# A transformer block on one core: the transposed input comes from TensorE, and every engine's order of work is rewritten

## What is computed

```
q, k, v = LN(x) @ Wq, LN(x) @ Wk, LN(x) @ Wv
P       = softmax(mask(q @ k.T) / 16)            # causal
x       = x + LN((P @ v) @ Wo)
i       = argmax(log_softmax(logits) + gumbel(u))   # one of 8 weights
x       = x + LN(LN(x) @ W[i] + b[i])
```

## Time and profile before

| | |
|---|---|
| median of three runs | 430.8 us |
| profiled execution | 428.95 us |
| its span, first to last instruction | 427.1 us |
| mean granted clock of TensorE | 0.975 |
| busy | PE 90%, DVE 77%, ACT 61%, POOL 51% |
| data moved | 67.75 MB, 159 GB/s |

### The profile page before, as it was taken

One profiled execution on the slowest core, in us unless ns is written; L12 is line 12 of the kernel. 1 busy time (PEld: TensorE's weight loads), 2 busy tenths in 40 slices (PEclk: granted clock), 3 DMA queues, 4 the chain that ended last, 5 costly groups with the idle time before them and its releaser, 6 DMA issues.

```text
span 427.1 us, 7846 instructions
## 1 busy us (share of the span) xinstructions
PE 384.1 (90%) x2652; PEld 359.5 (84%) x2652; DVE 330.9 (77%) x844; ACT 259.3 (61%) x642; POOL 216.0 (51%) x367
## 2 busy tenths in 40 slices
PE   7996967999869998999879998799979998999994
PEld 6775856999769996899769997699968997899994
DVE  4488755799847987789867998579868998667876
ACT  5866555576546665575655765567665757555642
POOL 5115264554645554645855446455656448535234
PEclk9998998999989998999999999899999999999998
DMA  6323884249843498328872498435982388331012
GB/s 196 119 55 122 240 221 115 69 171 254 229 130 103 193 240 238 115 69 271 232 190 81 163 262 243 126 114 199 272 219 82 120 241 237 105 107 51 25 51 74
DMA packets 45611, 67.75 MB, mean 159 GB/s; under 512 B 8196, under 2 KB 38276, under 8 KB 44676
## 3 DMA queue, kind: packets, MB, share of 16 engines
...
q10 hardware_dynamic: 272, 0.26, 0.2%
...
## 4 chain that ended last, share of the span: by engine, by line
PE 45%; DMA 26%; issue 9%; DVE 7%; ACT 4%; POOL 3%; POOLq 3%; SPq 3%; DVEq 0%
PE bank L1003 25%; PE score L1003 17%; DMA p_kept<-p_turn 16%; DMA p_turn<-p_kept 9%; ACT pT_hi L704 3%; SPq L443 3%; PE bank L1157 2%; POOLq L517 2%; DVE p_turn L911 2%; POOL pT_lo L546 1%; DMA x_kept<-x_turn 1%; DVE neg_scores L901 1%; DVE g_lo L767 1%; ACT g_hi L582 1%; PE bank L1128 1%
## 5 line engine op out<-in xcount | busy, mean ns | idle before, releaser
L546 POOL TENSOR_TENSOR pT_lo<-p_turn,pT_hi 128x128 fp32r<-128x128 f32 (+7 forms) x60 | 82.2, 1393 | 22.2 <-ACT pT_hi L704 22.1
L1003 PE MATMUL bank<-v_hi,pT_lo 128*128 128x258 f32 x288 | 82.6, 287 | 7.0 <-DVEq L865 3.9
L1003 PE MATMUL bank<-v_lo,pT_hi 128*128 128x258 f32 x288 | 81.6, 283 | 0.0
L1003 PE MATMUL bank<-v_hi,pT_hi 128*128 128x258 f32 x288 | 81.2, 282 | 0.0
L1003 PE MATMUL score<-xT_hi,g_lo 128*128 128x384 f32 (+4 forms) x176 | 65.0, 369 | 15.0 <-DVE neg_max L901 14.9
L503 POOL TENSOR_TENSOR o_rstd<-o_ss,minus_half 128x1 f32<-128x1 f32 x64 | 37.9, 594 | 77.4 <-ACT squares_junk L738 77.4
L695 ACT ACTIVATE probs<-neg_scores,neg_max 128x128 f32<-128x128 f32 (+3 forms) x64 | 49.2, 776 | 42.0 <-DVE neg_max L901 41.9
L1003 PE MATMUL score<-xT_hi,g_hi 128*128 128x384 f32 (+4 forms) x176 | 63.2, 359 | 0.0
L1003 PE MATMUL score<-xT_lo,g_hi 128*128 128x384 f32 (+4 forms) x176 | 63.2, 359 | 0.0
L1003 PEld LDWEIGHTS bank<-v_hi,pT_lo 128*128 128x128 f32 x288 | 54.7, 190 | 8.5 <-issue 6.9
L1003 PEld LDWEIGHTS bank<-v_lo,pT_hi 128*128 128x128 f32 x288 | 54.9, 191 | 0.6
...
## 6 DMA issues: line engine op xcount, KB each, us to landing
x_sb<-in_L_attn_x_dram SPq DMA_DIRECT2D x32, 256.0 KB, 5.4
out_dram<-f_sb SPq DMA_DIRECT2D x31, 256.0 KB, 5.6
x_kept<-x_turn SPq DMA_DIRECT2D x7, 1024.0 KB, 4.3
x_turn<-x_kept SPq DMA_DIRECT2D x28, 256.0 KB, 7.1
p_kept<-p_turn SPq DMA_DIRECT2D x7, 960.0 KB, 9.8
...
p_kept<-p_turn SPq DMA_DIRECT2D x7, 704.0 KB, 3.1
...
```

Source lines behind the costliest of these rows:

```text
L546: nc.gpsimd.tensor_tensor(p_half(pT_lo, n), p_quads(n), p_half(pT_hi, n).bitcast(f32), ALU.subtract).then_inc(p_lo_ready, 1)
L1003: last = nc.tensor.matmul(dst, l, r, start=(i == 0), stop=(i == len(passes) - 1))
```

## The change

X becomes a step of PE. For each pair of tiles of the next batch, four transposes with the identity go from `xn` into a PSUM bank; ACT rounds from there to `xT_hi`, DVE subtracts to `xT_lo` and releases the bank. The steps B, W and R go, and with them the DRAM tensor `x_kept` and the buffer `x_turn`. The jobs that share the four banks become 28 a batch. pT has four slots in place of three, numbered through the batches. G2 and G3 move behind S0 and S1 of the batch that uses them. The lists of all five engines are rewritten. The waits that counted whole batches now count the entries of the lists (`turned`, `rounded`, `reduced`), since the last batch has no block transposes for some tiles.

```diff
--- before.py
+++ after.py
@@ -54,10 +54,9 @@
-    PS = 3
+    PS = 4
...
-    PE_ORDER = """S0 S1 S2 S3 O6' O7' S4 Y1' V0 S5 Y2' F0' O0 S6 S7 O1 F1' V1 V2 Y3' F2' O2 V3 F3' O3 O4 O5 G0 G1 G2 Y0 G3"""
-    ACT_ORDER = """Y0' G3' E0 E1 E2 E3 O6' H0 O7' H1 P0 P1 Y1' E4 V0 H2 Y2' E5 O0 P2 F0' P3 H3 E6 O1 E7 V1 F1' V2 Y3' O2 P4
-        P5 V3 F2' O3 F3' X0 X1 O4 X2 X3 O5 G0 G1 P6 P7 G2"""
-    DVE_ORDER = """G2' M0 M1 G3' Q0 Q1 M2 Y0' M3 L0 L1 K0 K1 Q2 Q3 L2 K2 B0 R6' R7' M4 B1 Y1' Q4 V0 B2 M5 L3 F0' K3 Q5 Y2'
-        M6 N3' B3 Z0' M7 R0 R1 F1' Q6 V1 V2 Q7 Y3' F2' Z1' N0 R2 V3 F3' Z2' R3 N1 X0 X1 X2 X3 R4 R5 Z3'
-        G0 N2 G1"""
-    POOL_ORDER = """P7' L0 L1 C6' L2 C7' P0 P1 C0 L3 U0' P2 P3 N3' C1 U1' C2 P4 P5 U2' C3 N0 U3' N1 C4 C5 N2 P6"""
-    SP_ORDER = """P0 Q0 P1 A3' Q1 P2 W0 Z0' Q2 A0 R0 P3 Z1' Q3 A1 Z2' A2 Z3'"""
-    PE_LAST = """S0 V0 S1 S2 O6' S3 O7' Y1' S4 Y2' F0' O0 S5 Y3' S6 F1' V1 O1 V2 O2 V3 O3 F2' F3' T4 Y0 S7 Y1 T5 O4 T6 F0
-        O5 T7 O6 F1 Y2 O7 Y3 F2 F3 Y4 F4"""
-    ACT_LAST = """Y0' G3' E0 E1 E2 O6' E3 V0 O7' Y1' P0 P1 Y2' E4 O0 F0' Y3' E5 P2 P3 F1' V1 O1 V2 O2 V3 O3 F2' T4 Y0 E6
-        F3' Y1 T5 E7 O4 T6 F0 O5 T7 O6 Y2 F1 O7 Y3 Y4 F2 F3 F4"""
-    DVE_LAST = """G2' M0 Y0' G3' Q0 M1 M2 Q1 Q2 R6' M3 Q3 V0 Y1' R7' M4 Y2' F0' N3' M5 Y3' Z0' R0 M6 F1' V1 Z1' R1 V2 N0
-        R2 V3 R3 F2' N1 F3' T4 Y0 Z2' M7 Y1 T5 Z3' R4 T6 F0 Z0 R5 T7 N2 F1 R6 Y2 N3 Z1 Y3 R7 F2 N4 Y4 F3
-        F4 Z2 Z3 Z4"""
-    POOL_LAST = """P7' C6' C7' P0 P1 C0 N3' U0' P2 P3 U1' C1 C2 N0 C3 N1 U2' U3' C4 U0 C5 C6 N2 U1 N3 C7 N4 U2 U3 U4"""
-    SP_LAST = """P0 Q0 P1 Q1 Z0' Z1' Z2' Z3' Z0 Z1 Z2 Z3 Z4"""
+    PE_ORDER = """S0 S1 F1' G2' S2 S3 G3' O6' O7' V0 Y2' S4 V1 Y3' S5 V2 S6 O0 O1 S7 V3 X0 O2 O3 F2' X1 Y0 F3' X2 X3 G0 G1
+        Y1 F0 O4 O5"""
+    ACT_ORDER = """P6' E0 E1 P7' G2' F1' E2 E3 G3' H0 O6' H1 O7' V0 Y2' H2 P0 P1 V1 E4 Y3' P2 E5 V2 P3 O0 O1 E6 H3 V3 E7 X0
+        O2 O3 X1 Y0 F2' X2 X3 P4 P5 G0 G1 Y1 F3' F0 O4 O5"""
+    DVE_ORDER = """R4' M0 R5' M1 F1' L0 Q0 Q1 G2' K0 M2 L1 M3 Q2 N2' K1 G3' Q3 L2 Z1' K2 R6' R7' N3' V0 Y2' M4 V1 Q4 Y3' M5
+        L3 Q5 V2 M6 K3 R0 Q6 R1 M7 N0 V3 Q7 X0 R2 R3 F2' X1 Y0 F3' N1 X2 X3 Z2' G0 G1 Y1 F0 Z3' Z0"""
+    POOL_ORDER = """C5' P6' P7' L0 L1 U1' L2 C6' C7' N2' N3' P0 P1 P2 P3 C0 L3 C1 N0 C2 C3 U2' N1 P4 P5 U3' U0 C4"""
+    SP_ORDER = """Z0' A2' P0 Q0 P1 Z1' Q1 A3' P2 A0 Q2 P3 A1 Q3 Z2' Z3'"""
+    PE_LAST = """S0 G2' G3' V0 S1 S2 S3 O6' Y2' S4 O7' S5 F1' T4 O0 S6 O1 V1 Y3' S7 V2 T5 O2 O3 F2' F3' Y0 Y1 V3 O4 T6 O5
+        F0 T7 O6 F1 Y2 O7 Y3 F2 F3 Y4 F4"""
+    ACT_LAST = """E0 G2' P6' P7' G3' E1 E2 E3 O6' Y2' E4 V0 O7' P0 P1 E5 T4 O0 F1' P2 P3 O1 E6 V1 Y3' V2 T5 E7 O2 O3 F2'
+        Y0 Y1 F3' V3 O4 T6 O5 T7 F0 O6 Y2 F1 O7 Y3 Y4 F2 F3 F4"""
+    DVE_LAST = """R4' M0 R5' Q0 N2' G2' G3' M1 M2 Q1 Q2 M3 Q3 Y2' R6' M4 V0 R7' M5 N3' F1' T4 R0 M6 Z1' R1 N0 V1 Y3' M7 V2
+        T5 R2 R3 F2' N1 F3' Y0 Y1 Z2' V3 Z3' R4 T6 R5 F0 N2 T7 Z0 F1 R6 Y2 N3 Z1 Y3 R7 F2 N4 Y4 F3 F4 Z2
+        Z3 Z4"""
+    POOL_LAST = """C5' N2' P6' P7' C6' C7' P0 P1 N3' C0 U1' P2 C1 P3 N0 C2 C3 N1 U2' U3' C4 C5 N2 U0 C6 U1 N3 C7 N4 U2 U3
+        U4"""
+    SP_LAST = """Z0' P0 P1 Q0 Q1 Z1' Z2' Z3' Z0 Z1 Z2 Z3 Z4"""
...
-    AHEAD = {"L": 1, "K": 1, "H": 1, "B": 1, "X": 1, "G": 1, "W": 1, "R": 1, "A": 2}
+    AHEAD = {"A": 2}
-    def turns_of(text, ahead="LKHBXG"):
+    def turns_of(text, ahead="LKHXG"):
...
-            elif kind in "VOYFG":
+            elif kind in "VOYFXG":
...
-    x_kept = nc.dram_tensor("x_kept", (PART, QUADS, RUN), f32, kind="Internal").ap()
-        x_turn = sb("x_turn", [PART, QUADS * RUN])
-        x_turned = sem("x_turned")
...
+        def p_half(half, b, n):
+
+            return half[:, (b.known * NT + n) % PS, 0:(n + 1) * PART].rearrange("p (u i s) -> p u i s", i=QUADS, s=QUAD)
...
-                    elif kind == "W":
-
-                        sp.wait_ge(x_turned, b.count(NP, 0))
-                        sp.dma_start(x_kept.rearrange("p q r -> p (q r)"), x_turn[:, :]).then_inc(x_written, 16)
-                    elif kind == "R":
-                        sp.wait_ge(x_written, b.count(16, 0))
-                        fetch(x_turn[:, :], x_kept.rearrange("(i a) q r -> q a i r", i=QUADS), x_raw_loaded)
                     elif kind == "P":
 
-                        sp.wait_ge(p_turned, b.count(NT, 2 * n + 2))
+                        sp.wait_ge(p_turned, turned[(2 * n + 1, b.known)])
                         sp.dma_start(p_kept[n].rearrange("p q r -> p (q r)"), p_slot(n)).then_inc(p_written[n], 16)
                     elif kind == "Q":
-                        sp.wait_ge(p_written[n], b.count(16, 16))
+                        sp.wait_ge(p_written[n], 16 * (turned_pairs(b, n)))
...
             def normalise_x(b, p):
 
-                if b.known > 1:
-                    act.wait_ge(x_turned, b.count(NP, p + 1 - 2 * NP))
                 act.wait_ge(x_shift_ready, b.count(NP, p + 1))
...
+            def slot_read(b, n, kind):
+
+                free, at = (b, n - PS) if n >= PS else (b.other(-1), n + NT - PS)
+                if not free.exists() or follows(in_act, (kind, n, b.known), ("O", at, free.known)):
+                    return
+                if kind == "T" and follows(in_pe, ("T", n, b.known), ("O", at, free.known)):
+                    return
+                used = Job(free, "O", at)
+                act.wait_ge(bank_full[used.bank], used.used + 1)
...
-                        c, k = n // KC, n % KC
-                        if n == 0:
-                            act.wait_ge(x_raw_loaded, b.count(QUADS * 16, 0))
-                            act.wait_ge(scores_ready, b.count(NT, 0))
-                            for j in range(KC):
-                                nc.scalar.activation(xT_first[:, j, :].rearrange("p (i s) -> p i s", i=QUADS),
-                                                     raw_block(0, j)[:, 0], ACT.Identity)
-                        nc.scalar.activation(split_block(xT_hi, c, k), raw_block(c, k),
-                                             ACT.Identity).then_inc(x_hi_ready, 1)
+                        x_hi(Job(b, "X", n), n, x_hi_ready)
...
-            def x_blocks(b, p):
-
-                dve.wait_ge(xn_ready, b.count(NP, p + 1))
-                if b.known != 1 and p == 0 and not follows(in_dve, ("B", p, b.known), ("G", 3, b.known - 1)):
-                    for c in range(2):
-                        dve.wait_ge(x_lo_ready[c], b.count(KC, -KC))
-                turned = x_turn[:, :].rearrange("p (q k t s) -> p t k q s", q=QUADS, k=KC, t=NT)
-                for t in (2 * p, 2 * p + 1):
-                    last = nc.vector.transpose(turned[:, t], xn[:, t, :].rearrange("p (k q a) -> p k q a", k=KC, q=QUADS))
-                last.then_inc(x_turned, 1)
...
-                if full[(kind, n, 0)][1] == -1:
+                if full[(kind, n, 0)][1] < (kind in "XG"):
...
-                        dve.wait_ge(x_hi_ready, b.count(2 * KC, n + 1 - 2 * KC))
-                        c, k = n // KC, n % KC
-                        nc.vector.tensor_tensor(split_block(xT_lo, c, k), raw_block(c, k),
-                                                split_block(xT_hi, c, k).bitcast(f32), ALU.subtract
-                                                ).then_inc(x_lo_ready[c], 1)
-                    elif kind == "B":
-                        x_blocks(b, n)
+                        x_lo(Job(b, "X", n), n, x_hi_ready, b.count(NP, n + 1 - NP))
...
-            def x_transposes(job, p):
-
-                pe.wait_ge(xn_ready, p + 1)
+            def x_transposes(b, job, p):
+
+                pe.wait_ge(xn_ready, b.count(NP, p + 1))
...
-                        c = n // 2
-                        if n % 2 == 0:
-                            pe.wait_ge(x_lo_ready[c], b.count(KC, 0))
-                        g_quarter(Job(b, "G", n), [], n)
+                        g_quarter(Job(b, "G", n), [] if n % 2 else [Job(b, "X", n), Job(b, "X", n + 1)], n)
+                    elif kind == "X":
+                        x_transposes(b, Job(b, "X", n), n)
```

More of the change, by code:

```diff
@@ L191, in places_of, with counts_of, t_count @@
         return at
-    in_dve, in_act = places_of(DVE_ORDER, DVE_LAST), places_of(ACT_ORDER, ACT_LAST)
+    in_pe, in_act = places_of(PE_ORDER, PE_LAST), places_of(ACT_ORDER, ACT_LAST)
+    in_dve, in_pool = places_of(DVE_ORDER, DVE_LAST), places_of(POOL_ORDER, POOL_LAST)
     def follows(places, then, first):
         return first in places and places[first] < places[then]
+    def counts_of(places, wanted):
+        found = sorted((at, n, b) for (kind, n, b), at in places.items() if kind == wanted and 0 <= b < B)
+        return {(n, b): i + 1 for i, (_at, n, b) in enumerate(found)}
+    turned = counts_of(in_dve, "Q")
+    rounded, reduced = counts_of(in_act, "P"), counts_of(in_pool, "P")
+    turned_by_pe = counts_of(in_act, "T")
+    def t_count(b, n, g):
```

(54 more changed lines are left out.)

47 lines of the change are left out of this document (17 added, 30 removed).

## The result

The changed kernel takes **413.5 us** (median of 4, 410.79 to 415.11) against 430.99 (median of 4, 430.01 to 432.88): ratio 0.958, 95% interval 0.952 to 0.965. The forecast was 409.0 with a range of 399 to 424. The profiled execution took 414.19 us, its span 412.4. The four executions of the changed kernel differ with TensorE's clock: 410.79 us at a mean granted clock of 0.998, 415.11 at 0.986; the profiled one had 0.990.

The account below looks back on a forecast made before the run. PE, busy 90% of the span, was taken as the bound. 428.95 - 28.6 - 6.9 - 5.6 + 12.3 + 7.0 = 407.15 for the profiled execution, plus 1.85 to the median: 409.0 us, range 399 to 424.

Parts of the forecast that it names:

- PE's two steady waits, -28.6: PE's waits for `neg_max` (14.9 us) and `xT_lo` (11.5) both go, with 2.2 for the gaps: 28.6 us less.
- Clock stretches, -6.9: Four of PE's five low-clock stretches follow the removed steady waits and go with them, 1.7 us each: 6.9 us less.
- Rival 3: PE transposes in the close let the clock fall once a cycle: 12 us more, 421 us; chance 0.04.
- Batch 0, -5.6: PE's 3.95 us wait for the first probabilities goes with its clock stretch, as O0 moves later: 5.6 us less.
- Transposes, +12.3: On PE, 16 x transposes a batch at 0.44 us per group of four, seven batches: 12.3 us more.
- Slower than 0.1 us: Sign of being wrong: a PE transpose slower than 0.1 us, where 0.09 was read from the row.
- worth nothing by itself: Dropping DVE's x block transposes, 21.2 us of DVE, gains nothing alone, since DVE doesn't end last over a cycle.
- either way it fits: DRAM round trip from Q7's end takes about 12 us without x traffic, or 16.9 as now, against 18 allowed.
- the allowance of 18 us: Time from Q7's end allowed for the DRAM round trip, counting PE's work to O6' less 3.2 for P6'.
- only take away a wait: Four pT slots in place of three remove a wait and change nothing else; no time booked.
- New waits, +7.0: Small slacks in PE's close slip by 1.0 us a cycle over seven cycles: 7.0 us more.
- the hand-made table: New engine orders laid beside each other with profiled durations; slacks of 0.3 to 1 us at Y0, F3', G0, O4.

Follow-up runs that it names:

- e4: Kernel before with its old orders and three slots, only x made by PE transposes, DRAM transfers and DVE block transposes dropped; 412.9 us, ratio 0.957.
- e3: e5 with the x transfers of the kernel before put back as traffic nobody uses; 413.4 us, ratio 0.958 to the kernel before.
- e1: Changed kernel with one DVE step moved, Z2' from ahead of G0 to behind F0; 397.9 us, ratio 0.923 to the kernel before.
- e6: e1 with PE's X groups issued twice, 8 transposes instead of 4; 410.0 us, ratio 0.950 to the kernel before.
- e5: e1 with three pT slots instead of four; 404.4 us, ratio 0.936 to the kernel before.

## Why the prediction was right, and where not

The direction held, and 413.5 lies in the range, 4.5 above the forecast; the gain is 4% where 5% had been forecast. By its steps:

- **PE's two steady waits, -28.6.** Both went. The reason given was half wrong: the new place of M0 and G2 was credited beside the shorter trip, and e4 shows that the old orders lose the `neg_max` waits too once x leaves the DMA queue. e3 has none either, with the long trip under the new orders; there its cost comes up at O6' and V1.
- **Clock stretches, -6.9.** All five of the kernel before are gone, and two new ones came, one behind an O4 wait, one behind the late bias load in batch 0; e1's profile has none before its last 5 us. Rival 3, transposes that let the clock fall, has nothing for it: the changed kernel, e1 and e6 hold 1.00 through the close.
- **Batch 0, -5.6.** The wait for the first probabilities went, and the 2.5 us wait that had been left in went as well; two waits at X0 and X1 (2.2) took the place of the latter.
- **Transposes, +12.3.** e6: 12.1 by doubling, 11.1 for the groups as they stand. About right in sum, with 0.109 us for one and not 0.09. "Slower than 0.1 us" was among the signs of being wrong; it came, and nothing hung on it.
- **The x path's removal "worth nothing by itself".** That was said of DVE's 21.2 us, the busy time of the row (56 x 418 ns would be 23.4; the instructions overlap). No run tried DVE's side alone. The transfers, with their issue on SP, cost 9 us by e3 against e5.
- **Round trip, "either way it fits".** The trip itself came as said (write near 5, 4.6 measured), so this cost nothing here. But the allowance of 18 us was wrong, as e3 shows: it counted ACT and POOL for P6' up to O6', and not what waits behind P6' and P7' on POOL.
- **Four slots "only take away a wait".** Priced at nothing; some 5 us in these orders.
- **New waits, +7.0.** This is the term that missed. 11.4 were measured (10.4 and 6 x 0.16; 12.2 by the cycles), all at one place, G0's bank, where the hand-made table had one of its slacks under 1 us. The table gave Z2' its usual 0.9 us. It took 3.8, since in the new POOL order P4 and P5 start at the same moment. The sign was there to be read. This is step Z before (ns min/median/max, first and last start):

```profile
L979 DVE SCALAR_TENSOR_TENSOR f_sb<-f_sb,f_rstd,y x64: 469/478/1060, 94.2 to 424.1; 128x256 f32<-128x256 f32 x64
```

Six of these Z take about 1,050 ns, each beside a subtraction of POOL, and each ends 0.28 us after it.

So 407.15 + 4.4 (11.4 of waits for 7.0) + 1.7 (clock) + 1.5 (the later start) = 414.7, against 414.19 profiled. The fit is closer than its terms, and that is luck: the clock stretch at 25 us is not in it, nor that a cycle without waits is 45.87 us in e1 where 46.4 had been worked out, 3.2 less over six; the two pull opposite ways.

The mechanism that was forecast, PE as the bound, holds fully only in e1. e1 is 15 us below e4. That is what the new orders, the fourth slot and the right place for Z2' bring together; with three slots (e5) it is 8.5. In the change as made, one held DVE step at the wrong place gave it all back, which is why a full rewrite of the orders came out equal to dropping one DMA path. Between the profiles of e4 and e1 (15.5 us), six cycles shorter by 1.63 make 9.8; the first and the last batch together make 5.9, in which lie the wait in batch 0 of 3.6 that e4 keeps and the fallen clock behind it. The 1.63 lie at e4's X steps: from start to start the 16 transposes take 2.7 us there and 1.58 in e1, and the O passes beside them 13.6 and 13.0.
